# Two products per unit replaced by a mixing ahead of one product, in the last stage of a fused attention and channel-mixing kernel

## The chip, the cores and the metric

The kernel runs on one core of one Trainium2 chip. The time is the device time of one execution in microseconds. PE is TensorE, DVE is VectorE, ACT is ScalarE, POOL is GpSimd, SP issues the transfers.

## What is computed

The input x has 8 sequences of 512 tokens with 128 channels. Two blocks follow one another, each as x + layernorm(block(layernorm(x))). The first is a state-space attention with 32 heads. The second, cut to what matters here:

```
x_prev = x shifted by one token (zero ahead of the first)
xr = mu_r * x + (1 - mu_r) * x_prev
xk = mu_k * x + (1 - mu_k) * x_prev
r = sigmoid(xr @ W_r.T);  k_act = square(relu(xk @ W_k.T))
out = r * (k_act @ W_v.T)
```

mu_r and mu_k have one value per channel. All arithmetic on the chip here is fp32.

## The kernel before

Tokens are taken in 32 tiles: a chunk is 64 tokens of all 8 sequences, a tile is the 64 tokens of two sequences, so a chunk has four tiles (NQ = 4) and there are 8 chunks. Tile n = 4c + q. The attention runs over the tiles in a software pipeline: in its step n each engine works on neighbouring tiles, in an order written out by hand. All engines synchronize by semaphores, and each runs its instructions in program order.

- PE, step n: project_x(n+1) into x_ps (L859), turn(n+1) (L923), project_bc(n+2) (L851), y_turn(n-1) (L1045), mix(n) (L958, L946, L952), score(n+1) (L937), y_out(n-1) (L1054), then a part of the last stage, ffn(n).
- DVE, step n: gated_y(n-1) (y, L1397), state(n-1) (sp, L1386), mask(n) (sg, L1378), a part of the last stage, x of tile n+1 (weighted_x with a = 0, L1371), biased(n+2) (bc, L1354), xg of tile n+1 (L1371), rotations(n+2) (rot L1359, turned_bc L1364).
- ACT, step n: late_o(n-2), the silu of x_ps for tile n+1 (x_gate, L660), turned, copy_in, a part of the last stage, late_yt, squares, z_gate, late_ysq.
- POOL, step n: lower_part (x_lo), a part of the last stage, mse and rb (L450, L453), wx (L461), zs (L468), st (L476).

The last stage is the second block. It works in units: unit u is chunk u for u = 0 to 6, units 7 and 8 are the halves of chunk 7. It follows the attention with two chunks' distance: while chunk c is in the attention, unit c-2 is normalized (ACT, L724, at q = 1), transposed by PE (turn_normed, L1071, q = 2), copied by ACT out of PSUM twice at q = 3 (turned_x: curT, L739, and prevT, shifted by one token, L740), and PE makes the keys from them (project_k, end of step q = 3). POOL's carry writes the first column of prevT, the last token of the chunk before. One chunk later PE makes the receptances (project_r, q = 0) and the values (project_v, L1128, q = 1). The mixing weights mu and 1 - mu are multiplied into the weights once, so that keys and receptances are two products each, summed in PSUM:

```
nc.tensor.matmul(k_ps, w_cur[:, 0], cur[:, columns(u)], start=True, stop=False)
nc.tensor.matmul(k_ps, w_prev[:, 0], prev[:, columns(u)], start=False, stop=True)
...
nc.tensor.matmul(r_ps, cur[:, at_i], w_cur[:, 1], start=True, stop=False)
mm = nc.tensor.matmul(r_ps, prev[:, at_i], w_prev[:, 1], start=False, stop=True)
```

The profile gives the lines L1088 and L1091 to the keys, L1111 and L1112 to the receptances; each fp32 matmul leaves two records. The DVE part of the last stage: moments (agg L1461, fmo L1463) at q = 0, norm_biases (fnb, L1472) and last_residual (L1493) at q = 1, factor_terms (L1433 to L1437), gated_v (L1480) and stats3 (L1487) at q = 2, residual (L1444) and stats2 (L1450) at q = 3. POOL's rstd raises fmo to the power -1/2 (frs, L495) between fmo and fnb. After the last tile each engine runs last_ffn, with the remaining work of units 5 to 8 in an order of its own; DVE's begins with stats2(6), moments(6), factor_terms(7), gated_y(31), norm_biases(6).

Of the kernel before, what the change touches and what calls it, by code (L numbers as in the profile page):

```python
# [48 lines left out]

FAC_STEPS = 3  # L50
LAST_SPLIT = 2
UNITS = [(c * NQ, c * NQ + NQ) for c in range(NC_ - 1)] + [(NT - NQ, NT - NQ + LAST_SPLIT), (NT - NQ + LAST_SPLIT, NT)]

FLAG_AT = 6
# [32 lines left out]
def build(nc, x, w_in, a_log, dt_bias, bc_bias, w_out, w_r, w_k, w_v, mu, consts, out, force_general=False):  # L87
    ctx = ExitStack()
    with ctx:  # L89
        def sb(name, *shape, dt=F32):  # L90
            return ctx.enter_context(nc.sbuf_tensor(name, list(shape), dt))
# [142 lines left out]
        def flat(buf):  # L234
# [58 lines left out]
        cnames = ("x1 stats agg mom pow norm_bias normed tr_ps tr_sb carried shifted k_ps k_relu k_act r_ps th "  # L293
                  "v_ps f stats3 res outv").split()
        C = {n: sem("c_" + n) for n in cnames}
        s_mix = sem("mixing_weights")
# [4 lines left out]
        def valid(c):  # L301

            return 0 <= c < NC_
# [19 lines left out]
        def slots(u):  # L323
            return slice(slot(lo(u)), slot(hi(u) - 1) + 1)
# [80 lines left out]
        def _(pool):  # L405
# [4 lines left out]
            nc.gpsimd.memset(halfn[:], -0.5).then_inc(s_ones, 1)  # L410
            nc.gpsimd.memset(one[:], 1.0).then_inc(s_ones, 1)
            nc.gpsimd.memset(st[:], 0.0).then_inc(S["st_zero"], 1)
            nc.gpsimd.memset(curT[:], 0.0).then_inc(S["st_zero"], 1)
            pool.wait_ge(s_ones, 2)
            for k in range(NT // AK):
                pool.wait_ge(a_mo, (k + 1) * FIRST_MOM)
# [77 lines left out]
                t = slice(rounds[k][0], rounds[k][1])  # L494
                nc.gpsimd.tensor_tensor(frs[:, t], fmo[:, t], halfn[:, 0:t.stop - t.start], ALU.pow).then_inc(C["pow"], 1)  # L495

            def carry(c):

                if c == 0:
                    pool.wait_ge(S["st_zero"], 2)  # L500
                pool.wait_ge(C["tr_sb"], c)
                wait_past(pool, C["r_ps"], c - 1)
                to, of = c % 2 * B, (c + 1) % 2 * B
                nc.gpsimd.tensor_tensor(prevT[:, to:to + B, 0:1], curT[:, of:of + B, L - 1:L],
                                        one[:].unsqueeze(1).broadcast_to([128, B, 1]), ALU.mult).then_inc(C["carried"], 1)

            def pool_outputs(u, part):
# [7 lines left out]
            def ffn(n):  # L515
                c, q = divmod(n, NQ)
                if q == 0 and valid(c - 2):
                    rstd(c - 2)
                if q == 1 and valid(c - 2):
                    carry(c - 2)  # L520
                if q == 2 and valid(c - 1):
                    factors(c - 1)

            def last_ffn():
                rstd(6)
                carry(6)
                factors(7)
                rstd(7)
                factors(8)
                carry(7)  # L530
# [33 lines left out]
        def _(act):  # L564
# [162 lines left out]
            def gate_r(u):  # L727
# [2 lines left out]
                nc.scalar.activation(th[:, slots(u)].rearrange("p q d -> p (q d)"), ffn_bank("r", u)[:, 0:n_of(u) * D],  # L730
                                     ACT.Tanh, scale=0.5).then_inc(C["th"], 1)

            def turned_x(u):
                act.wait_ge(C["tr_ps"], u + 1)
                wait_past(act, C["carried"], chunk_of(u))
                wait_past(act, C["r_ps"], ahead(u) + 1)
                b = sequences(u)
                x_t = ffn_bank("t", u)[:, 0:n_of(u) * 128].rearrange("p (b l) -> p b l", l=L)
                nc.scalar.activation(curT[:, b], x_t, ACT.Copy).then_inc(C["tr_sb"], 1)  # L739
                nc.scalar.activation(prevT[:, b, 1:], x_t[:, :, 0:L - 1], ACT.Copy).then_inc(C["shifted"], 1)  # L740

            def k_relu(u):
                act.wait_ge(C["k_ps"], u + 1)
# [65 lines left out]
        def _(pe):  # L809
# [250 lines left out]
            def turn_normed(u):  # L1060
                pe.wait_ge(C["normed"], hi(u))
                if u == 0:
                    pe.wait_ge(S["weights"], 4)
                elif u < 6:
                    pe.wait_ge(C["f"], hi(u - 1))
                elif u < 8:
                    pe.wait_ge(S["sg_ready"], NT)
                else:
                    pe.wait_ge(C["shifted"], 8)
# [4 lines left out]
            def project_k(u, general, part=(0, 1)):  # L1074
                pe.wait_ge(C["tr_sb"], u + 1)
                if u == 0:
                    pe.wait_ge(s_mix, 6)
                elif u == 6:
                    pe.wait_ge(S["t_sb"], NT)
                    pe.wait_ge(S["y_ready"], NT)  # L1080
                elif u == 7:
                    pe.wait_ge(C["shifted"], 7)
# [6 lines left out]
                if 1 in part:  # L1089
                    pe.wait_ge(C["carried"], chunk_of(u) + 1)  # L1090
                    nc.tensor.matmul(k_ps, w_prev[:, 0], prev[:, columns(u)], start=False, stop=True)\  # L1091
                        .then_inc(C["k_ps"], 1)

            def project_r(u):
                pe.wait_ge(C["tr_sb"], u + 1)
                pe.wait_ge(C["shifted"], u + 1)
                pe.wait_ge(C["carried"], chunk_of(u) + 1)
                if u < 5:
                    pe.wait_ge(C["k_relu"], u + 1)
                elif u == 5:  # L1100
                    pe.wait_ge(S["bc_ready"], NT)
                    pe.wait_ge(S["z_silu"], NT)
                elif u == 6:
                    pe.wait_ge(C["th"], 6)
                elif u == 7:
                    pe.wait_ge(S["y_ready"], NT)
                else:
                    pe.wait_ge(C["th"], 8)
                for k, i in enumerate(range(lo(u), hi(u))):
                    r_ps, at_i = ffn_bank("r", u)[:, k * D:k * D + D], slice(slot(i) * 128, slot(i) * 128 + 128)  # L1110
                    nc.tensor.matmul(r_ps, cur[:, at_i], w_cur[:, 1], start=True, stop=False)  # L1111
                    mm = nc.tensor.matmul(r_ps, prev[:, at_i], w_prev[:, 1], start=False, stop=True)  # L1112
                mm.then_inc(C["r_ps"], 1)

            def project_v(u):
                pe.wait_ge(C["k_act"], u + 1)
                if u < 5:
# [82 lines left out]
        def _(dve):  # L1200
# [264 lines left out]
            def norm_biases(k):  # L1465
# [86 lines left out]
            def step(n, q, general):  # L1552
# [77 lines left out]
```

## Time and profile before

| what | us |
|---|---|
| median of 3 runs | 247.09 (246.23 to 247.74) |
| the profiled execution | 246.15 |
| its span in the profile | 244.3 |
| PE busy | 215.4 (88%) |
| DVE busy | 204.2 (84%) |
| ACT busy | 180.0 (74%) |
| POOL busy | 140.7 (58%) |

The span runs from the first to the last instruction of the profiled execution; 1.85 us of its time lie around it. A busy PE is one with a matmul in flight, so it is not PE at its peak.

### The profile page before, as it was taken

The page shows a single profiled execution, that of the slowest core. Times are in us where ns is not written, and L with a number is a line of the kernel's source. Part 1 is how long each engine was busy: PE and PEld are TensorE (multiplying, and loading weights), DVE is VectorE, ACT ScalarE, POOL GpSimd, SP SyncE. Part 2 cuts the span into 40 slices and gives each one's busy share as a digit, 9 for nine tenths or more (in the row PEclk, how much of TensorE's full clock was granted, in tenths as well). Part 3 has the DMA queues.
Part 4 walks back from the last instruction along what each step waited for, and adds up shares of the span by engine and source line. Part 5 has one row for each costly group of instructions (what it writes and reads, how often), then busy time and mean ns, then how long its engine had stood idle before and what let it go on. Part 6 is the DMA issues. An engine that isn't in the chain of part 4 may idle for free. (4 is left out here: it accounts for less than half of the span.)

```text
span 244.3 us, 6527 instructions
## 1 busy us (share of the span) xinstructions
PE 215.4 (88%) x1962; PEld 160.5 (66%) x1962; DVE 204.2 (84%) x646; ACT 180.0 (74%) x696; POOL 140.7 (58%) x243
## 2 busy tenths in 40 slices
PE   0896897589899989999999999999999999999930
PEld 0893443347667757668876887788688768757920
DVE  1789999986977998796899899989988996966880
ACT  2366766648887868877987799879879977969661
POOL 7434033745656867757575765867585756544430
PEclk9999799979999999999999999999999999999995
DMA  4980000000000000000000001000100010010123
GB/s 120 226 277 17 0 0 0 1 0 3 1 4 1 3 3 0 4 0 4 0 5 0 3 1 46 4 0 3 43 3 3 13 34 4 1 43 3 43 51 90
DMA packets 10199, 6.45 MB, mean 26 GB/s; under 512 B 864, under 2 KB 9856, under 8 KB 10160
## 3 DMA queue, kind: packets, MB, share of 16 engines
q1 hardware_dynamic: 10016, 5.77, 9.4%
q8 instruction: 18, 0.29, 0.5%
q0 software_dynamic: 144, 0.21, 0.4%
q14 instruction: 21, 0.17, 0.2%
HBM read 3.88 MB, written 2.10 MB: 24 GB/s over the span
## 5 line engine op out<-in xcount | busy, mean ns | idle before, releaser
L958 PE MATMUL bank<-x,sg 64*64 64x256 f32 x256 | 35.5, 397 | 0.0
L660 ACT ACTIVATE bank<-bank,rsn 128x512 f32<-128x512 f32 x32 | 21.1, 659 | 18.3 <-PE bank L859 18.3
L958 PE MATMUL bank<-xg,sg 64*64 64x256 f32 x256 | 33.5, 381 | 0.0
L1371 DVE TENSOR_TENSOR x<-bank,wx 128x512 f32<-128x512 f32 x32 | 21.8, 682 | 13.3 <-ACT bank L660 12.9
L946 PE MATMUL pair<-x,turned_bc 64*64 64x256 f32 x224 | 31.2, 398 | 0.0
L425 POOL TENSOR_TENSOR x_lo<-xnT_all,x_hi 128x128 fp32r<-128x128 f32 x32 | 14.6, 459 | 24.9 <-ACT x_hi L575 24.9
L453 POOL TENSOR_TENSOR rb<-mse,halfn 128x2 f32<-128x2 f32 x32 | 25.1, 786 | 2.5
L1054 PE MATMUL bank<-wo_sb,yt 128*128 128x128 f32 x128 | 22.8, 300 | 0.0
L495 POOL TENSOR_TENSOR frs<-fmo,halfn 128x8 f32<-128x8 f32 (+2 forms) x13 | 15.1, 1160 | 13.2 <-DVE fmo L1463 13.2
L958 PEld LDWEIGHTS bank<-xg,sg 64*64 64x64 f32 x256 | 18.2, 136 | 6.7 <-issue 0.7
L958 PEld LDWEIGHTS bank<-x,sg 64*64 64x64 f32 x256 | 15.4, 135 | 10.1 <-issue 6.1
L649 ACT ACTIVATE junk<-bank 128x64 f32<-128x64 f32 x64 | 13.9, 229 | 10.7 <-DVE bc L1354 8.6
L450 POOL TENSOR_TENSOR mse<-msb,eps_all 128x2 f32<-128x2 f32 x32 | 7.7, 241 | 24.4 <-ACT junk L651 24.4
L1371 DVE TENSOR_TENSOR xg<-bank,wx 128x512 f32<-128x512 f32 x32 | 21.7, 678 | 0.0
L468 POOL TENSOR_TENSOR zs<-zs,ec_all 128x256 f32<-128x256 f32 x32 | 21.4, 669 | 0.0
L952 PE MATMUL bank<-st,bt 64*64 64x256 f32 x128 | 19.8, 387 | 0.5 <-DVE o_all L1306 0.5
L859 PE MATMUL bank<-w_hi,x_hi 128*128 128x512 f32 x32 | 16.9, 527 | 3.7 <-DVE w_lo L1255 2.8
L937 PEld LDWEIGHTS pair<-bt 64*64 64x64 f32 x256 | 17.1, 133 | 4.4
L476 POOL TENSOR_TENSOR st<-sp,f_all 128x256 f32<-128x256 f32 x28 | 18.1, 648 | 1.5 <-DVE sp L1386 1.5
L1054 PEld LDWEIGHTS bank<-wo_sb,yt 128*128 128x128 f32 x128 | 16.7, 190 | 3.2 <-ACT yt L676 0.8
L937 PE MATMUL pair<-bt 64*64 64x64 f32 x256 | 18.1, 219 | 0.0
L1359 DVE TENSOR_TENSOR rot<-bc,cs_all 128x384 f32<-128x384 f32 x32 | 17.5, 548 | 0.0
(193 smaller groups left out, 725.6 us busy)
## 6 DMA issues: line engine op xcount, KB each, us to landing
x_all<-x SPq DMA_DIRECT2D x16, 128.0 KB, 3.8
out<-o_all SPq DMA_DIRECT2D x14, 128.0 KB, 2.4
cm<-consts SPq DMA_DIRECT2D x1, 640.0 KB, 6.6
w_sb<-w_in SPq DMA_DIRECT2D x1, 480.0 KB, 5.8
out<-o_all SPq DMA_DIRECT2D x4, 64.0 KB, 2.1
cm<-consts POOLq DMA_DIRECT2D x1, 128.0 KB, 3.9
wo_sb<-w_out SPq DMA_DIRECT2D x1, 128.0 KB, 4.8
bcb_sb<-bc_bias SPq DMA_DIRECT2D x1, 96.0 KB, 4.2
```

What stands on the lines that cost most here:

```text
L453: nc.gpsimd.tensor_tensor(rb[:, par], mse[:], halfn[:, 0:R], ALU.pow).then_inc(S["rb_ready"], 1)
L468: nc.gpsimd.tensor_tensor(zs[:, q].rearrange("p (h e) -> p h e", e=P), zs[:, q].rearrange("p (h e) -> p h e", e=P), at(ec_all, n).unsqueez ...
L476: nc.gpsimd.tensor_tensor(st[:, q].rearrange("p (h e) -> p h e", e=P), sp[:].rearrange("p (h e) -> p h e", e=P), at(f_all, i).unsqueeze(2) ...
L660: nc.scalar.activation(x_ps[:], x_ps[:], ACT.Silu, scale=rsn[:, par:par + 1]).then_inc(S["x_silu"], 1)
L859: mm = nc.tensor.matmul(x_ps[:], a[:, par], b[:, O_X:O_S], start=(k == 0), stop=(k == 2))
L937: mm = nc.tensor.matmul(scores[half(h), r], bt[half(r), par, r, half(h)], bt[half(r), par, 1 - r, half(h)], start=True, stop=True)
L946: mm = nc.tensor.matmul(p_ps[half(1 - h)], turned_bc[half(h), q, 2 * r], rx(x, r)[half(h)], start=(r == 0), stop=(r == R - 1))
L952: mm = nc.tensor.matmul(y_ps[par][half(h)], bt[half(1 - h), par, h, half(h)], state[half(1 - h)], start=True, stop=stop)
L958: mm = nc.tensor.matmul(y_ps[par][half(h)], sg[half(h), a, r], rx(x, r)[half(h)], start=start, stop=stop)
L1054: mm = nc.tensor.matmul(o_ps, yt[:, k], wo_sb[:, k], start=(k == 0), stop=(k == 1))
L1359: vec.tensor_tensor(rot[:], bc[:].rearrange("p (g a n) -> p g a n", g=G3, a=2).unsqueeze(3) .broadcast_to([128, G3, 2, 2, H]), at(cs_all, ...
L1371: vec.tensor_tensor((x1, xg)[a][:, par].rearrange("p (a e) -> p a e", e=P), x_ps[:].rearrange("p (a e) -> p a e", e=P), wx[:, par, a].unsq ...
```

## The change

For units 0 to 5 (MIX_UNITS = 6) the mixed tokens themselves are made, and keys and receptances are one product each with the plain weights. ACT, in the place of its two copies, writes (1 - mu_k) x and (1 - mu_r) x to a new tile behind, one column further on, so that column 0 holds the last token of the chunk before (carry_scaled on POOL copies column 64 there). DVE then makes mu x + behind from the transposed tokens in PSUM, twice: the tokens for keys go to curT, those for receptances to prevT. DVE does so at the end of step q = 3, behind xg and ahead of rotations. The products wait for both. Units 6 to 8 stay as they are; for unit 6, ACT makes one more small copy (last) and POOL carries once for units 7 and 8. The key products of unit 5, which stood on either side of y_turn(31) on PE, become one ahead of it. The cleared tile on POOL is behind instead of curT.

```
+MIX_UNITS = 6
...
+        behind = sb("behind", 128, 2 * B, L + 1)
...
+        def turned_ps(u):
+            return ffn_bank("t", u)[:, 0:n_of(u) * 128].rearrange("p (b l) -> p b l", l=L)
...
-            nc.gpsimd.memset(curT[:], 0.0).then_inc(S["st_zero"], 1)
+            nc.gpsimd.memset(behind[:], 0.0).then_inc(S["st_zero"], 1)
...
-            def carry(c):
...
+            def carry_scaled(c):
+
+                pool.wait_ge(C["mixed"], 2 * c)
+                nc.gpsimd.tensor_tensor(behind[:, :, 0:1], behind[:, :, L:L + 1],
+                                        one[:].unsqueeze(1).broadcast_to([128, 2 * B, 1]), ALU.mult).then_inc(C["carried"], 1)
+
+            def carry_last():
+
+                pool.wait_ge(C["tr_sb"], 1)
+                pool.wait_ge(C["r_ps"], 6)
+                nc.gpsimd.tensor_tensor(prevT[:, B:, 0:1], curT[:, 0:B, L - 1:L],
                                         one[:].unsqueeze(1).broadcast_to([128, B, 1]), ALU.mult).then_inc(C["carried"], 1)
...
                 if q == 3 and valid(c - 2):
-                    turned_x(c - 2)
+                    scaled_behind(c - 2)
...
+            def scaled_behind(u):
+                act.wait_ge(C["tr_ps"], u + 1)
+                wait_past(act, C["carried"], u)
+                if u == 0:
+                    act.wait_ge(s_mix, 1)
+                for m in range(2):
+                    nc.scalar.activation(behind[:, m * B:m * B + B, 1:], turned_ps(u), ACT.Identity,
+                                         scale=one_less_mu[:, 1 - m:2 - m]).then_inc(C["scaled"], 1)
+                if u == MIX_UNITS - 1:
+                    act.wait_ge(C["r_ps"], u)
+                    nc.scalar.activation(prevT[:, 0:B, 0:1], turned_ps(u)[:, :, L - 1:L], ACT.Copy).then_inc(C["last"], 1)
...
+            def tokens_there(u):
+                if u < MIX_UNITS:
+                    pe.wait_ge(C["mixed"], 2 * u + 2)
+                    return
...
-                if 0 in part:
-                    pe.wait_ge(C["shifted"], u + 1)
+                if u < MIX_UNITS:
+                    nc.tensor.matmul(k_ps, wk_sb[:], cur[:, columns(u)], start=True, stop=True).then_inc(C["k_ps"], 1)
+                else:
                     nc.tensor.matmul(k_ps, w_cur[:, 0], cur[:, columns(u)], start=True, stop=False)
...
-                    nc.tensor.matmul(r_ps, cur[:, at_i], w_cur[:, 1], start=True, stop=False)
-                    mm = nc.tensor.matmul(r_ps, prev[:, at_i], w_prev[:, 1], start=False, stop=True)
+                    if u < MIX_UNITS:
+                        mm = nc.tensor.matmul(r_ps, prev[:, at_i], wr_sb[:], start=True, stop=True)
+                    else:
...
             def last_ffn(general):
-                project_k(5, general, (0,))
+                project_k(5, general)
                 y_turn(NT - 1, 1)
-                project_k(5, general, (1,))
                 y_out(NT - 1)
...
+            def mix(u):
+
+                dve.wait_ge(C["scaled"], 2 * u + 2)
+                if u == MIX_UNITS - 1:
+                    dve.wait_ge(C["last"], 1)
+                for m, (to, used) in enumerate(((curT, "k_ps"), (prevT, "r_ps"))):
+                    wait_past(dve, C[used], ahead(u) + 1)
+                    vec.scalar_tensor_tensor(out=to[:, sequences(u)], in0=turned_ps(u), scalar=mu_sb[:, 1 - m:2 - m],
+                                             in1=behind[:, m * B:m * B + B, 0:L], op0=ALU.mult,
+                                             op1=ALU.add).then_inc(C["mixed"], 1)
...
                     weighted_x(n + 1, (q + 1) % 2, 1)
+                if q == NQ - 1 and valid(n // NQ - 2):
+                    mix(n // NQ - 2)
                 if within(n + 2):
                     rotations(n + 2, (q + 2) % NQ)
```

## Rows read from the trace of the kernel before

**Rows 1.** Busy time per stage: us, then busy us and (records) of each engine.
```profile
144.00:170.00 26.00, 26.00 (x281) 20.23 (x280) 24.89 (x77) 22.04 (x98) 17.45 (x32) 1.00 0.05 13
```

**Rows 2.** Timeline of PE, one round: start us, us, engine, line, operation.
```profile
152.29 1.02 PE L1088 MATMUL bank<-curT,w_cur 128*128 128x512 f32 x2
153.15 1.02 PE L1091 MATMUL bank<-prevT,w_prev 128*128 128x512 f32 x2
...
158.39 0.39 PE L1111 MATMUL bank<-w_cur,curT 128*128 128x128 f32 x2
...
160.10 0.48 PE L859 MATMUL bank<-w_hi,x_hi 128*128 128x512 f32 x1
```

**Rows 3.** Timeline of DVE, in several rounds (in brackets: idle before, and who ended it).
```profile
117.08 0.69 DVE L1371 TENSOR_TENSOR x<-bank,wx 128x512 f32<-128x512 f32 x1 [2.68 <-ACT bank L660]
...
148.29 1.89 DVE L1444 SCALAR_TENSOR_TENSOR x_all<-o_all,tokc,x_all 128x128 f32<-128x128 f32 x4
...
151.74 0.67 DVE L1371 TENSOR_TENSOR xg<-bank,wx 128x512 f32<-128x512 f32 x1
152.34 0.54 DVE L1359 TENSOR_TENSOR rot<-bc,cs_all 128x384 f32<-128x384 f32 x1
...
154.85 0.67 DVE L1463 TENSOR_SCALAR fmo<-fag 128x8 f32<-128x8 f32 x1
155.67 0.69 DVE L1371 TENSOR_TENSOR x<-bank,wx 128x512 f32<-128x512 f32 x1
...
161.82 0.69 DVE L1371 TENSOR_TENSOR x<-bank,wx 128x512 f32<-128x512 f32 x1 [0.72 <-ACT bank L660]
...
213.22 1.13 DVE L1444 SCALAR_TENSOR_TENSOR x_all<-o_all,tokc,x_all 128x128 f32<-128x128 f32 x4
```

**Rows 4.** Timeline of POOL and of ACT in the same round.
```profile
154.85 0.65 POOL L476 TENSOR_TENSOR st<-sp,f_all 128x256 f32<-128x256 f32 x1
...
161.13 0.66 ACT L660 ACTIVATE bank<-bank,rsn 128x512 f32<-128x512 f32 x1 [1.68 <-PE bank L859]
```

**Rows 5.** Single lines of DVE: count, duration ns min/median/max, first and last start.
```profile
L1371 DVE TENSOR_TENSOR xg<-bank,wx x32: 670/679/682, 45.5 to 212.6; 128x512 f32<-128x512 f32 x32
...
L1386 DVE TENSOR_TENSOR sp<-pair,st x28: 407/414/416, 54.4 to 198.3; 128x256 f32<-128x256 f32 x28
...
L1346 DVE TENSOR_SCALAR w_cur<-wk_sb,mu_sb x1: 279/279/279, 63.2 to 63.2; 128x128 f32<-128x128 f32 x1
...
L1347 DVE TENSOR_SCALAR wv_half<-wv_sb x1: 218/218/218, 63.6 to 63.6; 128x128 f32<-128x128 f32 x1
...
L1463 DVE TENSOR_SCALAR fmo<-fag x13: 168/170/671, 89.8 to 235.7; 128x8 f32<-128x8 f32 x5, 128x4 f32<-128x4 f32 x4, 128x2 f32<-128x2 f32 x4
```

**Rows 6.** Timeline of the tail: DVE, then ACT, then PE.
```profile
214.93 0.86 DVE L1450 BATCH_NORM_STATS2 fst<-x_all 128x6 f32<-128x128 f32 x4
...
218.58 0.17 DVE L1472 SCALAR_TENSOR_TENSOR fnb<-fag,frs 128x8 f32<-128x8 f32 x1 [0.70 <-POOL frs L495]
...
215.38 0.58 ACT L740 ACTIVATE prevT<-bank 128x504 f32<-128x504 f32 x1
...
222.36 0.60 ACT L740 ACTIVATE prevT<-pair 128x504 f32<-128x504 f32 x1
...
217.89 1.02 PE L1088 MATMUL bank<-curT,w_cur 128*128 128x512 f32 x2
...
221.15 0.65 PE L1071 MATMUL pair<-cm,dt_all 128*128 128x128 f32 x4 [0.46 <-ACT dt_all L724]
...
223.43 1.02 PE L1088 MATMUL bank<-curT,w_cur 128*128 128x512 f32 x2
```

**Rows 7.** Busy time per stretch; behind the five engines PE's granted clock.
```profile
45.91:49.32 3.41, 1.55 (x7) 1.11 (x8) 3.31 (x7) 2.62 (x11) 2.51 (x4) 1.00 0.00 0
49.32:52.73 3.41, 3.41 (x32) 1.77 (x33) 2.67 (x6) 1.70 (x10) 1.84 (x4) 0.50 0.00 0
...
86.87:90.28 3.41, 2.33 (x17) 1.63 (x12) 3.34 (x13) 2.83 (x15) 2.22 (x5) 1.00 0.00 0
```

More of the change, by code:

```diff
@@ L292, in build @@
         ff = sb("ff", 128, 2 * NQ, D)
-        cnames = ("x1 stats agg mom pow norm_bias normed tr_ps tr_sb carried shifted k_ps k_relu k_act r_ps th "
+        cnames = ("x1 stats agg mom pow norm_bias normed tr_ps tr_sb carried shifted scaled mixed last k_ps k_relu k_act r_ps th "
                   "v_ps f stats3 res outv").split()
@@ L495, in rstd @@
                 nc.gpsimd.tensor_tensor(frs[:, t], fmo[:, t], halfn[:, 0:t.stop - t.start], ALU.pow).then_inc(C["pow"], 1)
-            def carry(c):
[L499 to L504, printed above, removed]
+            def carry_scaled(c):
[6 more added lines that the diff above has]
+                nc.gpsimd.tensor_tensor(prevT[:, B:, 0:1], curT[:, 0:B, L - 1:L],
                                         one[:].unsqueeze(1).broadcast_to([128, B, 1]), ALU.mult).then_inc(C["carried"], 1)
@@ L518, in ffn @@
                     rstd(c - 2)
-                if q == 1 and valid(c - 2):
-                    carry(c - 2)
+                if q == 1 and 1 <= c - 2 < MIX_UNITS:
+                    carry_scaled(c - 2)
                 if q == 2 and valid(c - 1):
@@ L525, in last_ffn @@
                 rstd(6)
-                carry(6)
                 factors(7)
@@ L529, in last_ffn @@
                 factors(8)
-                carry(7)
+                carry_last()
                 rstd(8)
@@ L731, in gate_r @@
                                      ACT.Tanh, scale=0.5).then_inc(C["th"], 1)
+            def scaled_behind(u):
[9 more added lines that the diff above has]
+                    nc.scalar.activation(prevT[:, 0:B, 0:1], turned_ps(u)[:, :, L - 1:L], ACT.Copy).then_inc(C["last"], 1)
             def turned_x(u):
                 act.wait_ge(C["tr_ps"], u + 1)
-                wait_past(act, C["carried"], chunk_of(u))
                 wait_past(act, C["r_ps"], ahead(u) + 1)
                 b = sequences(u)
-                x_t = ffn_bank("t", u)[:, 0:n_of(u) * 128].rearrange("p (b l) -> p b l", l=L)
-                nc.scalar.activation(curT[:, b], x_t, ACT.Copy).then_inc(C["tr_sb"], 1)
-                nc.scalar.activation(prevT[:, b, 1:], x_t[:, :, 0:L - 1], ACT.Copy).then_inc(C["shifted"], 1)
+                nc.scalar.activation(curT[:, b], turned_ps(u), ACT.Copy).then_inc(C["tr_sb"], 1)
+                nc.scalar.activation(prevT[:, b, 1:], turned_ps(u)[:, :, 0:L - 1], ACT.Copy).then_inc(C["shifted"], 1)
             def k_relu(u):
@@ L1068, in turn_normed @@
                 else:
-                    pe.wait_ge(C["shifted"], 8)
+                    pe.wait_ge(C["shifted"], 2)
                 for k, i in enumerate(range(lo(u), hi(u))):
@@ L1072, in turn_normed, with project_k @@
                 mm.then_inc(C["tr_ps"], 1)
-            def project_k(u, general, part=(0, 1)):
-                pe.wait_ge(C["tr_sb"], u + 1)
-                if u == 0:
-                    pe.wait_ge(s_mix, 6)
-                elif u == 6:
+            def tokens_there(u):
+                if u < MIX_UNITS:
+                    pe.wait_ge(C["mixed"], 2 * u + 2)
+                    return
+                pe.wait_ge(C["tr_sb"], u - MIX_UNITS + 1)
+                pe.wait_ge(C["shifted"], u - MIX_UNITS + 1)
+                if u == MIX_UNITS:
+                    pe.wait_ge(C["last"], 1)
+                    pe.wait_ge(s_mix, 6)
+                else:
+                    pe.wait_ge(C["carried"], MIX_UNITS)
+            def project_k(u, general):
+                tokens_there(u)
+                if u == 6:
                     pe.wait_ge(S["t_sb"], NT)
@@ L1081, in project_k @@
                 elif u == 7:
-                    pe.wait_ge(C["shifted"], 7)
+                    pe.wait_ge(C["shifted"], 1)
                 elif u == 8:
@@ L1085, in project_k @@
                 k_ps = ffn_bank("k", u)[:, 0:n_of(u) * 128]
-                if 0 in part:
-                    pe.wait_ge(C["shifted"], u + 1)
+                if u < MIX_UNITS:
+                    nc.tensor.matmul(k_ps, wk_sb[:], cur[:, columns(u)], start=True, stop=True).then_inc(C["k_ps"], 1)
+                else:
                     nc.tensor.matmul(k_ps, w_cur[:, 0], cur[:, columns(u)], start=True, stop=False)
[L1089 to L1092, printed above, removed]
+                    nc.tensor.matmul(k_ps, w_prev[:, 0], prev[:, columns(u)], start=False, stop=True)                        .then_inc(C["k_ps"], 1)
             def project_r(u):
-                pe.wait_ge(C["tr_sb"], u + 1)
-                pe.wait_ge(C["shifted"], u + 1)
-                pe.wait_ge(C["carried"], chunk_of(u) + 1)
+                tokens_there(u)
                 if u < 5:
@@ L1110, in project_r @@
                     r_ps, at_i = ffn_bank("r", u)[:, k * D:k * D + D], slice(slot(i) * 128, slot(i) * 128 + 128)
-                    nc.tensor.matmul(r_ps, cur[:, at_i], w_cur[:, 1], start=True, stop=False)
-                    mm = nc.tensor.matmul(r_ps, prev[:, at_i], w_prev[:, 1], start=False, stop=True)
+                    if u < MIX_UNITS:
+                        mm = nc.tensor.matmul(r_ps, prev[:, at_i], wr_sb[:], start=True, stop=True)
+                    else:
+                        nc.tensor.matmul(r_ps, cur[:, at_i], w_cur[:, 1], start=True, stop=False)
+                        mm = nc.tensor.matmul(r_ps, prev[:, at_i], w_prev[:, 1], start=False, stop=True)
                 mm.then_inc(C["r_ps"], 1)
@@ L1116, in project_v @@
                 pe.wait_ge(C["k_act"], u + 1)
+                if u == 0:
+                    pe.wait_ge(s_mix, 6)
                 if u < 5:
```

## The prediction

> **What bounds the kernel now.** I read the busy time by stage first [rows 1]: in the middle PE has matmuls in flight all the time, and DVE is busy 24.89 of 26 us, so neither has much to give. Busy shares can't say which of two full engines leads, so next came the timelines of one round of four tiles (one chunk, 22.4 us) on PE and DVE. On PE the last stage's products stand in the open: the two key products start at 152.29 and 153.15, the receptance products fill 158.39 to 160.10 [rows 2]. On DVE the only waits of a round are 0.72 us before x of the second tile (at 161.82) [rows 3], ended by ACT's silu, which itself had waited 1.68 us for PE's projection [rows 4], and some 0.15 us between fmo (ends at 155.52) and x at 155.67. So PE leads by 0.87 us in 22.4. More room on DVE is only in the first such round, 2.68 us at 117.08 [rows 3], and, by the same reading, in the last. Then the tail, where neither is full: the last unit's moments (DVE from 214.93), a power on POOL, fnb at 218.58, the normalized tokens on ACT, PE's transposes at 221.15 after 0.46 us idle, and from there PE almost without a gap to its end [rows 6].
>
> **PE's saving.** A key product of 512 columns costs 153.15 - 152.29 = 0.86 us; one of the two goes. The eight pairs of receptance records take 158.39 to 160.10, 1.71 us; half goes, 0.86. So 1.72 us a unit for six units, 10.3 us of PE work. That is the gain if nothing else became late.
>
> **DVE's cost.** Two scalar_tensor_tensor of 128x512, first input PSUM, second SBUF. The nearest row is xg, the same size and the same kinds of input: 679 ns, from its start to the next instruction 152.34 - 151.74 = 0.60 us [rows 3, 5]. The per-partition scalar adds 279 - 218 = 61 ns at 128x128 [rows 5]. So 0.66 to 0.67 us each from start to start, 1.34 a unit; bounds 1.20 (scalar free) and 1.50 (full durations of 0.74 do not overlap). Could POOL slow them? Instructions of this kind with two SBUF inputs (the residuals) take 1.89 us for four at 148.29, beside POOL's work, and 1.13 at 213.22, without it [rows 3]. But sp, one input PSUM and one SBUF, stays within 407 to 416 ns over 28 places, POOL at work or not [rows 5], so I take no slowing. The Trainium skill (GPSIMD Engine Reference, 1. Specifications) says that the SBUF interfaces are shared and that DVE contends when it has two SBUF inputs; mixing has one, and by the rule too it is spared, while the residuals are not, and the trace agrees (1.89 against 1.13).
>
> **A refund on DVE.** fmo takes 0.67 us at 154.85, against a median of 170 ns, and ends just after POOL's st [rows 3 to 5]. POOL's zs and st there follow from DVE's bc and sp. bc stands ahead of the mixing and sp is 0.7 us of DVE work before fmo, so after the change DVE comes to fmo 1.34 us later and st ends only some 0.3 later: fmo drops to about 0.17, 0.5 us back. Net on DVE: +0.84 a round; bounds +0.7 and +1.5.
>
> **Rounds with mixing.** PE's key product now waits for the second mix. Before, the next projection could start 1.6 us after xg ended (152.41 to 154.0); now 1.34 + 0.06 + 0.86 = 2.26, so PE is 0.66 later, and idle about 1.5 us ahead of the product, an idle that wasn't there. The receptance half, 0.86, comes back one tile later: PE then stands at -0.2. DVE has +0.84 against its 0.87 of waits: -0.03. So a steady round costs nothing to within 0.2 us, and PE's 1.72 us turn into waiting: the saved product is paid by the wait in front of it. Where DVE had room (the first round and the last) PE's -0.2 shows. Sum over units 0 to 4: -0.4 us (bounds -0.8 and +2.2: 1.5 instead of 1.34 and no refund give +0.66 more in each of four rounds). ACT writes two tiles as before, with a scale from SBUF: 0.60 us for the copy, 0.66 for the silu of the same size that has one [rows 4, 6]; +0.06 each, and ACT idles in front of PE's projection anyway. The Trainium skill (ScalarE: Activation LUTs, What ACT_TABLE_LOAD costs) puts a pointer operand at some 93 ns; these rows show some 60. By the page the sum would be 0.1 us longer, in the tail alone. POOL's carry moves to another tile, 0.2 us as before, behind mixes that are long done. The clearing of behind instead of curT is the same size.
>
> **The tail, unit 5.** Here mixing waits for ACT. ACT can't start on the turned tokens before o_all and its square, its second copy starts at 215.38 [rows 6] and ends near 215.96; with two scales and the small third instruction (some 0.2 us) ready at about 216.2. DVE would be free at 214.93. In order behind the mixing stand stats2(6), its moments, the next gated_y and fnb. So stats2(6) starts at 216.25 + 1.35 = 217.6 instead of 214.93: +2.67 (bounds 2.4 and 3.0). The key product itself doesn't care: its place on PE is 217.89 [rows 6]. Everything behind fnb keeps the 2.67: normalized tokens, transposes at 223.8 instead of 221.15. After them the receptances of unit 5 save 0.86 on PE, but the keys of unit 6 now wait for ACT's prevT: it started at 222.36 and ended at 222.96, PE was there at 223.43 [rows 6], so 0.45 of the 0.86 counts. Tail: +2.2 (bounds 1.7 and 2.7).
>
> **The clock.** PE would lie nearly idle from 218.4 to 223.8, with one pair of transposes and one small pair of products in between. In the kernel before the granted clock was halved after a stretch with PE busy 1.55 of 3.41 us (granted 0.50 in the next, 1.2 instead of 2.4 GHz), and stayed whole with 2.33 of 3.41 [rows 7]. The new gap is emptier than the first, so a fall is likely. At half clock the transposes (+0.4 us) and the products of unit 5 and 6 behind them take double, less 0.45 that would have waited for ACT: +0.8, bounds 0 and 1.7.
>
> **Sum.** Against the profiled execution: -0.4 + 2.2 + 0.8 = +2.6 on 246.15, so 248.8. It lies 0.94 below the median of the runs shown; +2.6 on 247.09 gives 249.7.
>
> **Rivals.** A measurement of this kernel can tell about 1%, 2.5 us, from no change: bounds 244.6 and 249.6.
> (a) The same without a fall of the clock in the tail: 247.09 + 1.8 = 248.9. For it: two small bursts break the gap; where it falls depends on chance.
> (b) DVE becomes the plain bound of the rounds: no refund at fmo, mixing 1.5. +0.66 in four rounds: 249.7 + 2.6 = 252.3. For it: only 0.87 us of waits in 22.4 are there to absorb 1.34. Against: POOL's order follows DVE's.
> (c) The idle 1.5 us in front of each key product pulls the clock down in the rounds. PE busy is then 1.9 of 3.4 at worst, between the two rows that I have [rows 7], so the trace doesn't exclude it. Each fall costs up to 1.5 us, two to four of them: 253 to 256.
> (d) The other side: the residuals of two SBUF inputs fall out of step with POOL. Four take 1.89 where 1.13 would do [rows 3]; with the last residuals, of the same form, that is twice 0.76 a round, in four rounds up to -6.1. It decides from 0.65 us a round, where it pays the tail off: at half the effect 246.7, at the full 243.6. Against: before both residuals POOL's chain hangs on DVE's own bc, factors and fmo, which shift with it.
> (e) The tail's wait is smaller than it looks, since the moments' chain has slack that I don't see: 247.3. Against: 0.46 us of idle on PE ended by ACT's tokens is all the slack that there is.
> That the change doesn't do as it says would show as more matmul records than are said below; the code has one product for units 0 to 5 plainly.
>
> **How the numbers follow.** Forecast 0.42, (a) 0.23, (b) 0.11, (c) 0.09, (d) 0.07, (e) 0.08. Likeliest time 249.7. The range takes in (a), (b) and (e), and cuts off most of (c) and the full (d): 246.8 to 253.0. Over 1% slower: half and a little more of the forecast's own spread (0.24, since 249.7 stands on the bound, and of (a) 0.07), (b), (c): 0.51. Over 1% faster: the strong half of (d): 0.04. Within: 0.45.
>
> **What would show it.** Key products of units 0 to 5: one pair of records each, with 1.4 to 1.6 us of PE idle in front of five of them, released by DVE's curT or prevT; receptance records for w_cur and w_prev only for units 6 to 8. Twelve mixing instructions near 740 ns. fmo of 8 columns under 0.3 us where it was 0.67. No DVE idle above 0.3 us before x in the steady rounds, and the round still 22.4 us: between x of tiles 18 and 26 44.8 us, as before. In the tail a wait of about 1.3 us of DVE on ACT's behind, and stats2(6) 2.3 to 2.7 us later; after it a stretch with granted clock 0.5. I am wrong if rounds grow by over 0.3 us (then b or c; the clock row tells which), if residuals beside POOL fall towards 1.13 (d), or if transposes of unit 6 come less than 2 us late (e).

## The result and the profile after

The kernel with the change takes 251.58 us, the median of 4 runs (250.91 to 252.75); the kernel before took 246.76 beside it (4 runs, 246.23 to 247.74). The ratio is 1.0196, with a 95% interval of 1.0154 to 1.0238: slower, by 4.8 us where 2.6 were forecast. The time lies inside the range. The profiled execution took 250.91 us with a span of 248.9, against 246.15 and 244.3 before.

The instructions are the ones that the change names. By line, with busy us and mean ns, then idle time before them:

```profile
L746 ACT ACTIVATE behind<-bank,one_less_mu 128x512 f32<-128x512 f32 x12 | 7.6, 695 | 0.0
...
L1509 DVE SCALAR_TENSOR_TENSOR curT<-bank,mu_sb,behind 128x512 f32<-128x512 f32 x6 | 4.4, 740 | 1.3 <-ACT behind L746 1.3
L1509 DVE SCALAR_TENSOR_TENSOR prevT<-bank,mu_sb,behind 128x512 f32<-128x512 f32 x6 | 4.4, 739 | 0.0
...
L1490 DVE TENSOR_SCALAR fmo<-fag 128x8 f32<-128x8 f32 x5 | 0.9, 172 | 0.2
...
L1114 PE MATMUL bank<-curT,wk_sb 128*128 128x512 f32 x12 | 6.7, 636 | 6.5 <-DVE prevT L1509 6.5
```

Twelve mixes near 740 ns, one pair of key records a unit, PE waiting 6.5 us for tokens, fmo at 172 ns: the parts came out near their prices.

Where the 4.6 us of span arose can be read from the starts of DVE's x instructions, one in each tile (x of tile 12 stands just ahead of the first mixing), and of the last values product on PE:

| us | before | after | difference |
|---|---|---|---|
| x of tile 12 | 106.19 | 106.06 | -0.13 |
| 12 to 14 (first round with mixing) | 10.89 | 11.18 | +0.29 |
| 14 to 30 (four steady rounds) | 89.49 | 90.54 | +1.05 |
| 30 to 31 | 5.46 | 5.46 | 0 |
| x of 31 to PE's last product (tail) | 21.52 | 24.95 | +3.43 |

So the rounds cost 1.3 us where -0.4 stood in the prediction, and the tail 3.4 where 3.0 stood (2.2 for the wait, 0.8 for the clock). Between x of tiles 18 and 26 lie 45.28 us (139.87 to 185.15), not the 44.8 of before that the prediction gave as a sign.

**One round.** The timeline of PE after, which answers to [rows 2]: the key product (L1114) waits 1.29 us for the second mix. New is the second wait, 0.20 us at 156.25: the turn of tile 21 (L940) waits for DVE's sg.

```profile
154.23 1.13 PE L1114 MATMUL bank<-curT,wk_sb 128*128 128x512 f32 x2 [1.29 <-DVE prevT L1509]
155.66 0.40 PE L876 MATMUL bank<-w_hi,x_lo 128*128 128x512 f32 x1
...
156.25 0.41 PE L940 MATMUL pair<-cm,turned_bc 128*128 128x128 f32 x2 [0.20 <-DVE sg L1405]
...
160.78 0.48 PE L876 MATMUL bank<-w_hi,x_hi 128*128 128x512 f32 x1
```

Before, the turn came 0.23 us behind the last product of the projection and waited for nothing; now it comes 0.59 us behind it (156.25 against 155.66):

```profile
154.48 0.39 PE L859 MATMUL bank<-w_hi,x_lo 128*128 128x512 f32 x1
154.71 0.38 PE L923 MATMUL pair<-cm,turned_bc 128*128 128x128 f32 x2
```

The timeline of DVE after, which answers to [rows 3]:

```profile
152.18 0.68 DVE L1398 TENSOR_TENSOR xg<-bank,wx 128x512 f32<-128x512 f32 x1
152.78 0.74 DVE L1509 SCALAR_TENSOR_TENSOR curT<-bank,mu_sb,behind 128x512 f32<-128x512 f32 x1
153.44 0.74 DVE L1509 SCALAR_TENSOR_TENSOR prevT<-bank,mu_sb,behind 128x512 f32<-128x512 f32 x1
154.09 0.55 DVE L1386 TENSOR_TENSOR rot<-bc,cs_all 128x384 f32<-128x384 f32 x1
...
155.70 0.41 DVE L1405 TENSOR_TENSOR sg<-pair,cm 128x256 f32<-128x256 f32 x1
...
156.69 0.17 DVE L1490 TENSOR_SCALAR fmo<-fag 128x8 f32<-128x8 f32 x1
156.85 0.69 DVE L1398 TENSOR_TENSOR x<-bank,wx 128x512 f32<-128x512 f32 x1
...
159.42 0.42 DVE L1424 TENSOR_TENSOR y<-bank,zs 128x256 f32<-128x256 f32 x1 [0.16 <-PE bank L975]
...
160.50 2.05 DVE L1531 SCALAR_TENSOR_TENSOR o_all<-ff,frs,x_all 128x128 f32<-128x128 f32 x4
162.51 0.69 DVE L1398 TENSOR_TENSOR x<-bank,wx 128x512 f32<-128x512 f32 x1
```

DVE is full: 0.66 and 0.65 us for the mixes, fmo at 0.17, no idle before either x, and x of tile 22 at 162.51, with DVE idle only 0.16 us before y (159.42), for PE's score. Counted from start to start the wait costs 0.24 to 0.25 us: y follows x of its tile by 2.57 us here (156.85 to 159.42), and by 2.33 where it waits for nothing (162.51 to 164.84). It closes a loop: the mixes push sg back, turn and everything behind it on PE wait for sg, and DVE's own next y waits for PE.

**The tail.** DVE, answering to [rows 6]: the mixing waits 1.30 us for ACT, stats2(6) starts at 218.85 instead of 214.93.

```profile
217.52 0.75 DVE L1509 SCALAR_TENSOR_TENSOR curT<-bank,mu_sb,behind 128x512 f32<-128x512 f32 x1 [1.30 <-ACT behind L746]
...
218.85 0.86 DVE L1477 BATCH_NORM_STATS2 fst<-x_all 128x6 f32<-128x128 f32 x4
...
222.50 0.17 DVE L1499 SCALAR_TENSOR_TENSOR fnb<-fag,frs 128x8 f32<-128x8 f32 x1 [0.97 <-POOL frs L500]
```

PE: two short bursts after the key product, and the transposes at 225.07 instead of 221.15.

```profile
219.10 1.02 PE L1114 MATMUL bank<-curT,wk_sb 128*128 128x512 f32 x2
...
221.59 0.44 PE L1062 MATMUL bank<-cm,y 128*128 128x128 f32 x2 [1.47 <-DVE y L1424]
...
223.91 0.71 PE L1071 MATMUL bank<-wo_sb,yt 128*128 128x128 f32 x4 [1.87 <-ACT yt L683]
...
225.07 0.86 PE L1088 MATMUL pair<-cm,dt_all 128*128 128x128 f32 x4 [0.46 <-ACT dt_all L731]
...
225.73 1.92 PE L1135 MATMUL bank<-wr_sb,prevT 128*128 128x128 f32 x8
```

Busy time in stretches, with PE's granted clock behind the five engines (answering to [rows 1, 7]). In the middle the clock stays at 1.00; in the tail it is halved after a stretch with PE busy 1.06 of 3.39 us.

```profile
148.00:170.00 22.00, 20.51 (x220) 15.47 (x218) 21.67 (x66) 18.48 (x81) 14.95 (x27) 1.00 0.06 14
...
222.00:225.39 3.39, 1.06 (x8) 0.84 (x8) 2.23 (x11) 2.68 (x11) 1.68 (x3) 1.00 0.00 0
225.39:228.81 3.42, 3.42 (x14) 2.72 (x12) 2.26 (x13) 3.25 (x8) 1.27 (x4) 0.50 0.00 0
228.81:232.00 3.19, 3.19 (x23) 2.54 (x22) 1.00 (x6) 2.02 (x6) 2.87 (x5) 1.00 0.00 0
```

### The profile page after: what moved, and what is told of

It is laid out like the page before. It is cut to its first block and busy times, and to the rows that moved or that the text cites. A ratio compares the mean times of both kernels' runs of the same rounds, so it can differ in the third digit from the quotient of the medians.

```text
span 248.9 us, 6407 instructions
## 1 busy us (share of the span) xinstructions
PE 208.7 (84%) x1902; PEld 153.9 (62%) x1902; DVE 212.0 (85%) x658; ACT 181.5 (73%) x697; POOL 142.1 (57%) x241
## 5 line engine op out<-in xcount | busy, mean ns | idle before, releaser
L975 PE MATMUL bank<-xg,sg 64*64 64x256 f32 x256 | 33.0, 376 | 0.0
L1398 DVE TENSOR_TENSOR x<-bank,wx 128x512 f32<-128x512 f32 x32 | 21.9, 683 | 7.5 <-ACT bank L667 7.4
L473 POOL TENSOR_TENSOR zs<-zs,ec_all 128x256 f32<-128x256 f32 x32 | 22.0, 686 | 0.0
L1398 DVE TENSOR_TENSOR xg<-bank,wx 128x512 f32<-128x512 f32 x32 | 21.8, 680 | 0.0
L940 PE MATMUL pair<-cm,turned_bc 128*128 128x128 f32 x64 | 12.9, 284 | 6.7 <-DVE sg L1405 6.7
```

Of the source, the lines that this page charges most:

```text
L473: nc.gpsimd.tensor_tensor(zs[:, q].rearrange("p (h e) -> p h e", e=P), zs[:, q].rearrange("p (h e) -> p h e", e=P), at(ec_all, n).unsqueez ...
L975: mm = nc.tensor.matmul(y_ps[par][half(h)], sg[half(h), a, r], rx(x, r)[half(h)], start=start, stop=stop)
L1398: vec.tensor_tensor((x1, xg)[a][:, par].rearrange("p (a e) -> p a e", e=P), x_ps[:].rearrange("p (a e) -> p a e", e=P), wx[:, par, a].unsq ...
```

## The experiments

All edits are to the kernel after, but for the control. Ratios are to the kernel before in the same runs (medians 246.21, 246.89 and 246.85 in the three groups of runs: the first four, the next three, the last two); a ratio can differ by 0.001 from the quotient of the two medians. "Tail" is the time from x of tile 31 to PE's last product, "round" that between x of tiles 18 and 22, as in the table.

**1. Unit 5 keeps its two products.**

```
-MIX_UNITS = 6
+MIX_UNITS = 5
...
-                project_k(5, general)
+                project_k(5, general, (0,))
                 y_turn(NT - 1, 1)
+                project_k(5, general, (1,))
```

(turned_x, the carry for unit 6 and the counts follow from it.)

> Unit 5 keeps its two products (ACT copies, DVE does not mix it); units 0 to 4 are mixed. Theory (a wait in the tail and a clock fall behind it): of the 4.6 us that the span grew, 3.4 belong to unit 5, so this one lies 1.2 us over the kernel before (ratio 1.005) and x of tile 31 stays at the changed kernel's place, near 213.2; no half clock between 225 and 229. Rival (the products and mixing of the rounds carry the loss): 3.5 us or more over the kernel before, ratio 1.014.

Measured: 247.41 us, ratio 1.005 (1.0024 to 1.0075). The tail is 21.48 us again (before 21.52), the granted clock in it 1.00 throughout; x of tile 31 is at 213.27, as after (213.24). What remains slower is the rounds' part. So the tail's 3.4 us belong to the change of unit 5: its mixing, and what it moves on ACT and PE. Experiment 2 tells these apart.

**2. All six units mixed, but DVE mixes unit 5 behind the moments of unit 6.**

```
-                if q == NQ - 1 and valid(n // NQ - 2):
+                if q == NQ - 1 and 0 <= n // NQ - 2 < MIX_UNITS - 1:
                     mix(n // NQ - 2)
...
                 moments(6)
+                mix(5)
                 factor_terms(7)
```

> DVE mixes unit 5 behind stats2(6) and moments(6) instead of ahead of them; nothing else moves. Theory: the wait for ACT is filled and stats2(6) starts at once behind the last mask; the power on POOL runs beside the mixing. The transposes of unit 6 come 2 us earlier than in the changed kernel, PE's gap is too short for a clock fall, and 2.5 to 3 us come back: ratio to the kernel before 1.007 to 1.009. Rival (the wait is only moved, since gated_y of the last tile stands behind the mixing anyway): under 1 us comes back, ratio 1.016.

Measured: 247.66, ratio 1.0057 (1.0029 to 1.0085), a little better than expected. DVE's timeline in the tail, then PE's: the mixing no longer waits for ACT, since it comes when ACT is done, and the transposes stand 9.40 us behind x of tile 31 (before 9.12, after 11.83).

```profile
216.33 0.86 DVE L1477 BATCH_NORM_STATS2 fst<-x_all 128x6 f32<-128x128 f32 x4
...
218.18 0.75 DVE L1509 SCALAR_TENSOR_TENSOR curT<-bank,mu_sb,behind 128x512 f32<-128x512 f32 x1
...
220.27 0.16 DVE L1499 SCALAR_TENSOR_TENSOR fnb<-fag,frs 128x8 f32<-128x8 f32 x1
...
222.83 0.66 PE L1088 MATMUL pair<-cm,dt_all 128*128 128x128 f32 x4 [0.46 <-ACT dt_all L731]
```

The tail is 21.45 us: same work, another place in DVE's queue, 3.5 us (2.5 to 3 were expected). The clock falls nowhere in it. It was the order that cost.

**3. PE kept busy in the tail,** with products of 512 and 256 columns that nobody reads, before and behind y_turn(31); the mixing's place is that of the change.

```
                 project_k(5, general)
+                filler(512, 256)
                 y_turn(NT - 1, 1)
+                filler(512, 256)
                 y_out(NT - 1)
```

> The changed kernel with PE filled by products of constants into an idle bank, 768 columns behind the keys of unit 5 and 768 behind the last y_turn, both inside PE's idle stretches of the tail; all waits stay. Theory: no half clock in the tail, transposes of unit 6 at the same place, the end 0.7 to 1.1 us earlier (ratio to the kernel before 1.016). Rival (the half clock lies beside ACT's work and costs nothing): the end within 0.2 us of the changed kernel's.

Measured: 249.89, ratio 1.0139 (1.0113 to 1.0165). PE's timeline: the fillers, then the transposes, as late as after the change (11.84 us behind x of tile 31), and the receptances of unit 5, which started at 225.73 after and went at half clock.

```profile
220.37 1.45 PE L1145 MATMUL pair<-cm 128*128 128x512 f32 x4
...
222.29 1.46 PE L1145 MATMUL pair<-cm 128*128 128x512 f32 x4
...
225.49 0.66 PE L1088 MATMUL pair<-cm,dt_all 128*128 128x128 f32 x4 [0.46 <-ACT dt_all L731]
225.98 1.06 PE L1135 MATMUL bank<-wr_sb,prevT 128*128 128x128 f32 x8
```

```profile
225.50:229.00 3.50, 3.14 (x16) 2.21 (x17) 2.56 (x14) 3.50 (x10) 1.37 (x3) 1.00 0.00 0
```

Eight receptance records take 1.06 us where they took 1.92, the clock stays at 1.00 and the tail is 23.89 instead of 24.95. So the fall of the clock is worth 1.06 us, and the wait for the mixing with what hangs on it the rest: 3.43 - 1.06 = 2.37.

**4. One mix instead of two in units 0 to 4** (the receptances of these units take the tokens mixed for the keys).

```
-                for m, (to, used) in enumerate(((curT, "k_ps"), (prevT, "r_ps"))):
+                for m, (to, used) in list(enumerate(((curT, "k_ps"), (prevT, "r_ps"))))[0:1 if u < MIX_UNITS - 1 else 2]:
```

> For units 0 to 4 DVE makes only the mixed tokens of the keys; the second mixing is left out and the receptances are computed from the keys' tokens, so the output is not the reference's. Unit 5 as in the changed kernel. Theory (in the rounds DVE's own instructions and PE's wait for them set the pace): a round from x to x is 22.64 us in the changed kernel; 0.66 less DVE work in each makes DVE's sum 21.8, PE's key product starts 0.66 earlier, and the round is 21.9 to 22.1; x of tile 31 some 2.5 to 3 us earlier than in the changed kernel. Rival (the round is set by PE's issue of the remaining matmuls, not by the mixing): the round stays within 0.2 us of 22.64.

Measured: 247.1, ratio 1.0037 (1.0003 to 1.007). Rounds shrink from 22.64 to 21.88 us, x of tile 31 comes at 209.61 instead of 213.24, 3.6 us earlier where 2.5 to 3 were expected. One mix is 0.66 us of DVE; 0.76 a round comes back, 0.66 for the mix and 0.09 because DVE's wait before y falls from 0.16 to 0.07. So a steady round of the changed kernel shrinks by what DVE is spared. But PE's wait for the tokens shrinks with it, from 6.5 to 3.3 us in all, so this run alone does not tell the two apart. The tail is 25.62 us, longer than after: its granted clock is 0.50 over 6.83 us (219.61 to 226.44), twice as long as after, which hides part of the 3.6 us. Why it stays low for longer is open.

**5. PE's order: with experiment 2, project_bc goes ahead of turn at q = 0,** that is where turn waits for sg.

```
-                if n + 1 < NT:
+                if n + 1 < NT and not (q == 0 and n >= 12):
                     turn(n + 1, (n + 1) % NQ)
                 if n + 2 < NT:
                     project_bc(n + 2, par)
+                if n + 1 < NT and (q == 0 and n >= 12):
+                    turn(n + 1, (n + 1) % NQ)
```

> On top of the tail order of the run before (ratio 1.0057): at q = 0, PE makes project_bc(n+2) ahead of turn(n+1) instead of behind it. Theory (in the changed kernel turn waits for DVE's mask, which the mixing has pushed back, and PE loses some 0.35 us there each round; DVE's y then waits 0.16 us for PE): no wait for sg ahead of the turn at q = 0, and the round shrinks from 22.64 to 22.4 us, ratio about 1.002. Rival (DVE's own instructions are the bound and PE's loss costs nothing): the round stays at 22.6 and the ratio at 1.005 to 1.006.

Measured: 245.71, ratio 0.9948 (0.9922 to 0.9973); the round is 22.24 us instead of 22.64, where 22.4 was expected. PE's timeline: the projection L868 now fills the time before turn, which starts without a wait. DVE's: no idle at y any more, and x of tile 22 waits 0.21 us for ACT's silu instead, as it did before the change.

```profile
155.82 0.36 PE L868 MATMUL bank<-w_hi,x_lo 128*128 128x448 f32 x1
156.02 0.38 PE L940 MATMUL pair<-cm,turned_bc 128*128 128x128 f32 x2
...
161.63 0.69 DVE L1400 TENSOR_TENSOR x<-bank,wx 128x512 f32<-128x512 f32 x1 [0.21 <-ACT bank L667]
```

More came back than the wait itself. Counted from x of tile 18, y starts 0.25 us earlier than after (19.30 against 19.55); and the last residuals, DVE's o_all, are shorter:

```profile
159.76 1.66 DVE L1533 SCALAR_TENSOR_TENSOR o_all<-ff,frs,x_all 128x128 f32<-128x128 f32 x4
```

1.66 us where the change had 2.05 (L1531, above), with another offset to POOL: its wx starts 0.40 us behind them (160.16), where after the change it started 0.04 ahead (160.46 against 160.50). They start 0.26 us earlier (20.37 against 20.63) and end 1.66 us later (22.03), where after the change the next x followed 2.01 us behind their start (22.64): -0.26 - 0.35 + 0.21 for the new wait is -0.40, the whole difference of the round. The first part is what the wait had cost; experiment 8 shows where the second comes from.

**6. With 5, the mixing ahead of xg.**

```
+                if q == NQ - 1 and 0 <= n // NQ - 2 < MIX_UNITS - 1:
+                    mix(n // NQ - 2)
                 if within(n + 1):
                     weighted_x(n + 1, (q + 1) % 2, 1)
-                if q == NQ - 1 and 0 <= n // NQ - 2 < MIX_UNITS - 1:
-                    mix(n // NQ - 2)
```

> On top of that: DVE mixes ahead of xg instead of behind it, so PE's key product can start 0.6 us earlier, while DVE's work stays the same. Theory (with PE's lost time already back, DVE's own work is the bound): the round stays within 0.1 us of the version before it, PE idles more in front of the projection or the turn instead of the key product. Rival (PE's wait for the tokens is the bound): another 0.3 to 0.5 us a round, ratio below 1.000.

Measured: 245.14, ratio 0.9927 (0.9902 to 0.9953), an interval that overlaps that of 5. PE's wait for the tokens falls from 6.5 to 3.6 us in all, while turn waits for sg 10 times instead of 5, and the round is 22.30 (22.24 in 5). That looks as if PE's idle in front of the key product cost nothing. But the residuals are long again:

```profile
159.61 2.09 DVE L1533 SCALAR_TENSOR_TENSOR o_all<-ff,frs,x_all 128x128 f32<-128x128 f32 x4
```

Against 5 they start 0.08 us earlier and the wait of 0.21 before x is gone, but the next x follows them by 2.01 us instead of 1.66: -0.08 - 0.21 + 0.35 = +0.06. DVE idles before no x in this round, so DVE's own work is its bound, as expected; what the earlier product gave went into longer residuals. Where those are short in both runs (1.30 and 1.28 us, between x of tiles 26 and 30), and where there are none (x of 12 to 14), the rounds fell, from 22.22 to 22.02 and from 10.78 to 10.57. So PE's wait for the tokens is not free: some 0.6 us less of it gave 0.2 us where PE leads, and the steady rounds do not separate it from the residuals.

**7. With 2, DVE keeps one mix; the receptances' is made by ACT and POOL.** ACT writes mu x to prevT, POOL adds behind.

```
+                if u < MIX_UNITS - 1:
+                    wait_past(act, C["r_ps"], ahead(u) + 1)
+                    nc.scalar.activation(prevT[:, sequences(u)], turned_ps(u), ACT.Identity,
+                                         scale=mu_sb[:, 0:1]).then_inc(C["half"], 1)
...
+            def mix_r(u):
+
+                pool.wait_ge(C["scaled"], 2 * u + 2)
+                pool.wait_ge(C["half"], u + 1)
+                b = sequences(u)
+                nc.gpsimd.tensor_tensor(prevT[:, b], prevT[:, b], behind[:, B:, 0:L], ALU.add).then_inc(C["r_mixed"], 1)
```

> On top of the tail order: for units 0 to 4 DVE mixes the keys' tokens alone; the receptances' are mixed without DVE, by a third ACT activation (mu_r x, out of PSUM) and an addition of 128x512 on POOL. The output is the reference's. Theory (DVE's second mixing is what the rounds pay for): rounds as with the keys mixed alone, 21.9 to 22.1 us, x of tile 31 near 209.8, the end 2 to 2.5 us ahead of the kernel before, ratio 0.990. Rivals: POOL's 1.3 us addition holds up its own mse, rb and wx, or slows DVE's residuals; then the round is back at 22.4 or more and the ratio 1.000 to 1.01.

Measured: 244.87, ratio 0.9924 (0.9895 to 0.9953), and a round of 22.15 us: 0.49 less than after where the mix was 0.66, and a little more than the 21.9 to 22.1 expected. POOL's timeline, then PE's: the sum takes 1.18 us on POOL, and turn still waits for sg.

```profile
151.43 1.18 POOL L514 TENSOR_TENSOR prevT<-prevT,behind 128x512 f32<-128x512 f32 x1 [1.34 <-ACT prevT L760]
...
154.57 0.41 PE L954 MATMUL pair<-cm,turned_bc 128*128 128x128 f32 x2 [0.38 <-DVE sg L1426]
```

The three activations have a price as well: PE waits 0.56 us in each round for ACT's yt (L1085), which it did not do in the steady rounds after the change.

**8. The control: the kernel before with the order of 5 on PE.**

> Control: the kernel before with nothing but PE's other order at q = 0 (project_bc ahead of turn). Theory (the turn's wait for the mask arose only because mixing moved the mask back): PE never waits there, so nothing comes back: ratio 1.000 within the interval, rounds 22.4 us, x of tile 31 at the place of the kernel before. Rival (the order itself is better, whatever the mixing): rounds of 22.1 us or less and a ratio of 0.993.

Measured: 246.95, ratio 1.0015 (0.9989 to 1.004), round 22.38 (before 22.39). Without the mixing the order is worth nothing to the round. But inside the round something moved, in DVE's timeline:

```profile
159.18 1.65 DVE L1495 SCALAR_TENSOR_TENSOR o_all<-ff,frs,x_all 128x128 f32<-128x128 f32 x4
161.94 0.69 DVE L1373 TENSOR_TENSOR x<-bank,wx 128x512 f32<-128x512 f32 x1 [1.11 <-ACT bank L660]
```

The residuals take 1.65 us, where they took 2.04 before (at 159.06), and DVE's wait before x grows by the same 0.39, from 0.72 to 1.11: here PE sets the round, so a shorter DVE only waits longer. The short residuals thus come with PE's order and not from the mixing. So the gain of 5 has two parts. The wait that the change had made is the 0.26; alone it would bring the round back to some 22.38 (an estimate, 22.64 - 0.26), the round of before. That 5 lies below this comes from the residuals, 0.35 less the new wait of 0.21.

**9. Both: 7 with the order of 5.**

> The run before with POOL's addition (ratio 0.9924, rounds of 22.15 us, PE waits 0.38 us for the mask ahead of the turn at q = 0) and PE's other order at q = 0. Theory (the two savings hit different waits): the wait for the mask goes, rounds 21.8 to 21.9, end 1.0 to 1.5 us earlier, ratio 0.987. Rival (with one mixing less, DVE is no longer late enough for the order to matter): the ratio stays at 0.992.

Measured: 242.06, ratio 0.9816 (0.9769 to 0.9863), faster than both kernels and than expected (0.987). The round is 21.59 us, where 21.8 to 21.9 were expected. DVE's timeline: x of two steady rounds, without idle before either.

```profile
158.97 0.69 DVE L1421 TENSOR_TENSOR x<-bank,wx 128x512 f32<-128x512 f32 x1
...
180.55 0.69 DVE L1421 TENSOR_TENSOR x<-bank,wx 128x512 f32<-128x512 f32 x1
```

Between x of tiles 12 and 31 lie 101.92 us against 105.84 before, -3.9; the tail is 21.47 (before 21.52). DVE does 0.66 us less in a round than in 5, and the round falls by 0.65. Against 7 the round falls by 0.56 us, and the same two parts are in it: DVE's wait for PE before y is gone, and the residuals take 1.65 us instead of 2.04.

## Why the prediction was right, and where it was off

- **PE's saving and PE's wait.** The products go as counted, and PE waits 1.29 us in front of five key products (1.4 to 1.6 were named). That the saving turns into waiting is what these rows show. Experiment 4 takes one mix away and the round follows. Experiment 6 shortens the wait and its steady rounds do not follow, but there the residuals grew, so that the wait itself costs nothing is not shown.
- **DVE's cost and the refund.** 0.66 and 0.65 from start to start, fmo 0.17: as priced. The mixes take 740 ns (679 for xg and 61 for the scalar). In this kernel POOL runs only mse and rb beside them, instructions that do not slow the residuals either; experiment 7 is the better witness: there the mix at 151.58 runs beside POOL's addition of two SBUF inputs (151.43 to 152.61) and takes 0.74 us as well, while rot behind it, with two SBUF inputs, takes 0.79 us instead of 0.55. In the steady round DVE's own work is 22.64 - 0.25 = 22.39 us after. Before it was 22.39 less the two waits of 0.72 and 0.15, 21.52. The difference, 0.87, is the +0.84 of the prediction. One reading of it was too narrow: in the round from x of tile 22 before the change, fmo took 0.17 us as well (177.25) and DVE waited 0.63 us for the next x instead, in a round of 22.38. So fmo's 0.67 us stood inside a wait, and the refund and DVE's waits are one sum.
- **The step that failed: "The receptance half, 0.86, comes back one tile later: PE then stands at -0.2".** It counted PE's work, not what PE's next step waits for. The mixes also push back sg, and turn waits for it. After the change turn starts 0.59 us behind the projection's product at 155.66, where before it came 0.23 us behind the same product; 0.36 us are lost. The projection is also 0.13 us later than priced: it starts 0.79 us later behind x of tile 12 (3.46 against 2.67), where 0.66 stood. (The 154.0 of the prediction is 153.15 + 0.86; the record has the projection start at 153.60.) So PE stands at 0.79 + 0.36 - 0.86 = +0.29, not at -0.2. In steady rounds that comes out as 0.25 at DVE's y: -0.03 + 0.25 = +0.22, measured +0.25 to +0.28 each. In the first round and the last PE leads (DVE still idles 1.62 us before x of tile 14 and 0.69 before x of tile 30): measured +0.29 and +0.26, where the prediction had -0.2 in each. The rounds' term was mis-sized by this: -0.4 in the sum, +1.3 measured, inside its bounds of -0.8 and +2.2. Those had been drawn for longer mixes and no refund, and neither came, so that the bounds held is luck. The signs set for being wrong did not show it either: growth of 0.25 to 0.28 us a round stayed just under the 0.3 that was named. Experiments 5 and 8 show the step: without the wait DVE reaches y 0.25 us earlier and the residuals 0.26 us earlier, and in the kernel without the mixing there is no such wait to take away.
- **The tail's wait.** stats2(6) comes 2.71 us later relative to x of tile 31 (2.67 predicted), transposes too (11.83 against 9.12). Behind them the saved product gives back 0.34 (0.45 predicted; 2.71 - 2.37). Experiment 2 shows that it is the place of the mixing in DVE's order.
- **The clock.** It fell where the prediction put it; price 1.06 us (3), 0.8 predicted, 1.7 the bound.
- **The rivals.** (a) no fall: false, the clock row shows it. (b) DVE as plain bound without refund: false in its conditions (refund there, mixing 0.66), but DVE is nearly full after the change all the same: it waits only before y, and one mix less gives 0.76 a round (4). (c) fall in the rounds: false, granted 1.00 from 148 to 170. (d) in the changed kernel false: the residuals took 2.05 us in the steady rounds; yet it is a real lever, 0.35 us a round in 5 and 0.39 in the control, where it only lengthened a wait. (e) slack in the tail: false, the transposes keep the whole delay.
- **The sum.** -0.4 + 2.2 + 0.8 = 2.6 predicted; 1.3 + 2.4 + 1.06 - 0.13 = 4.6 measured. Of the 2.0 us between, 1.7 are the rounds. The chances put "slower by over 1%" first and the time is inside the range; the likeliest value was 1.9 us too low. The direction and the tail came by the mechanism that was named; the rounds' share did not.

## What to carry to other kernels

When a product is replaced by elementwise work ahead of it, list what else the elementwise engine owes the matrix engine behind the new instructions: here the mask, which stands behind the mixed tokens, cost most of what the rounds lost, and one swap of two independent steps on PE gave it back. Run such a swap on the kernel before too and read its rows, not only its time: here that showed which part of the gain belonged to the change. Work that waits for a late producer belongs behind everything that others wait for: the same two instructions cost 3.5 us more ahead of the moments than behind them. Such a trade pays once the added work lies where there is time for it; with half of it on ACT and POOL, and the two orders mended, it made the kernel 1.8% faster instead of 2.0% slower.

## What the hardware showed unexpectedly

- **A scale from SBUF on ACT cost some 91 ns, not the 60 that I read from two unlike rows.** Writing 128x512 from PSUM took a mean of 604 ns before (L739, Copy) and 695 with the scale per partition (L746, Identity, to rows of 65 columns). The Trainium skill (ScalarE: Activation LUTs, What ACT_TABLE_LOAD costs) says some 93 ns for a pointer operand; the trace agrees with it within 2 ns, and my row was too far off.
- **The clock in the rounds withstood 1.3 us of idle PE in each of them,** and in experiment 1 a tail with PE busy 3.00 of 3.40 us; it fell after 1.06 of 3.39. In experiment 4 it stayed at half for 6.83 us. Why it lasted twice as long there is open.
- **The slowing of DVE beside POOL depends on the offset by amounts that matter:** the same four residuals took 2.05 and 1.66 us in steady rounds of two kernels (after, and 5), and 1.14 in the tail. In the steady rounds at 1.65 us (5, 8, 9) POOL's wx starts 0.30 to 0.41 us behind the first of them, in those at 2.03 to 2.09 at most 0.26 behind it. One residual takes 340 to 350 ns beside POOL's rb (128x2) and up to 718 beside zs or st (128x256). No run sets the offset by itself, so that it is the cause is read from rows and not shown.
